# DLRM tower on one core: in the last round one more feature by comparing and multiplying, and half of layer 2 moved behind the last products

## What is computed

```python
e = jnp.stack([tbl_0[ids[:, 0]], ..., tbl_25[ids[:, 25]]], axis=1)        # 2048 x 26 x 128
combined = jnp.concatenate([dense[:, None, :], e], axis=1)                # 27 vectors of a sample
inter = jnp.einsum('bnd,bmd->bnm', combined, combined)[:, TRIU_I, TRIU_J] # 351 products
h = jnp.concatenate([dense, inter, dense], axis=1)
h = jnp.maximum(h @ W_top1 + b_top1, 0.0)                                 # 512 wide
h = jnp.maximum(h @ W_top2 + b_top2, 0.0)                                 # 256 wide
y = h @ W_top3                                                            # one number
```

## Time and profile before

| | us |
|---|---|
| median of 3 runs | 474.87 (474.09 to 474.97) |
| the profiled execution | 477.4 |
| its span on the core | 475.4 |
| PE busy | 416.0 (87%) |
| DVE busy | 337.1 (71%) |
| ACT busy | 214.8 (45%) |
| POOL busy | 399.9 (84%) |

### The profile page before, as it was taken

The page is one execution under the profiler, slowest core; times in us unless marked ns, Lnnn a source line. Parts: engine busy times, 40 slices in busy tenths (PEclk is TensorE's granted clock), DMA queues, the critical chain, the costliest instruction groups (busy, mean ns, idle before and its releaser), DMA issues.

```text
span 475.4 us, 11713 instructions
## 1 busy us (share of the span) xinstructions
PE 416.0 (87%) x4210; PEld 391.8 (82%) x4210; DVE 337.1 (71%) x777; ACT 214.8 (45%) x719; POOL 399.9 (84%) x553
## 2 busy tenths in 40 slices
PE   0546786989999998999999989999699969989898
PEld 0436785989998998989898989999598969879786
DVE  3649878798698858786878769886588846844360
ACT  1044265454555344545544554555245453525352
POOL 7999999899899898998998989989989899899500
PEclk9978898889999999999999999999899998989999
DMA  7984413622221321323133313132132313121100
GB/s 174 219 206 128 114 43 79 160 65 71 72 78 42 79 80 46 78 72 85 41 79 76 80 42 83 48 84 65 40 84 73 79 45 79 44 74 41 29 2 0
DMA packets 19682, 36.58 MB, mean 77 GB/s; under 512 B 7823, under 2 KB 10391, under 8 KB 19630
## 3 DMA queue, kind: packets, MB, share of 16 engines
q0 software_dynamic: 8704, 17.84, 16.7%
q1 hardware_dynamic: 10926, 18.04, 13.3%
HBM read 35.85 MB, written 0.01 MB: 75 GB/s over the span
## 4 chain that ended last, share of the span: by engine, by line
POOL 61%; issue 25%; PE 8%; DMA 1%; POOLq 1%; DVE 1%; ACT 1%; DVEq 0%; ACTq 0%
POOL rows L408 34%; POOL y_wide L397 27%; PE dots_ps L467 2%; PE mlp_ps L506 2%; DMA rows<-in_tbl,idx_sb 1%; DVE inter L866 1%; POOLq L396 1%; PE late_ps L570 1%; PE mlp_ps L515 1%; PE turn_ps L548 1%; PE mlp_ps L557 1%; PE dots_ps L548 1%; ACT inter L690 1%; DMA idx_sb<-in_ids 0%; PE turn_ps L443 0%
## 5 line engine op out<-in xcount | busy, mean ns | idle before, releaser
L408 POOL DMA_INDIRECT rows<-in_tbl,idx_sb x272 | 265.9, 977 | 45.6 <-POOL y_wide L397 43.8
L818 DVE TENSOR_TENSOR onehot<-ids_sb,late_ps 125x1024 fp32r<-125x1024 int32 (+2 forms) x154 | 167.2, 1141 | 10.5 <-DMA ids_sb<-in_ids_by_round 6.5
L866 DVE COPY_PREDICATED inter<-mask,dots_ps 27x48 f32<-27x48 int32 x496 | 103.0, 208 | 79.1 <-ACT inter L690 62.6
L690 ACT COPY inter<-dots_ps 27x64 f32<-27x64 f32 x496 | 99.0, 200 | 92.4 <-PE dots_ps L467 58.7
L397 POOL MEMSET y_wide<- 64x448 f32 x272 | 133.9, 492 | 0.2
L467 PE MATMUL dots_ps<-vecs 128*64 128x54 f32 x1984 | 118.0, 225 | 1.9 <-issue 1.0
L467 PEld LDWEIGHTS dots_ps<-vecs 128*64 128x64 f32 x1984 | 114.0, 140 | 6.5 <-issue 3.4
L483 PE MATMUL turn_ps<-onehot,t_hi 125*128 125x256 f32 x378 | 100.5, 302 | 11.4 <-DVE vecs L646 11.4
L483 PE MATMUL turn_ps<-onehot,t_lo 125*128 125x256 f32 x378 | 96.0, 291 | 0.0
L483 PEld LDWEIGHTS turn_ps<-onehot,t_hi 125*128 125x128 f32 x378 | 75.2, 199 | 15.8 <-issue 10.0
L483 PE MATMUL late_ps<-onehot,t_hi 125*128 125x256 f32 x214 | 60.1, 314 | 22.1 <-DVE t_lo L831 17.2
(11 more groups left out here) (84 smaller groups left out, 364.2 us busy)
## 6 DMA issues: line engine op xcount, KB each, us to landing
ids_sb<-in_ids_by_round SPq DMA_DIRECT2D x25, 375.0 KB
...
```

The lines of the kernel that those rows point to most:

```text
L408: nc.gpsimd.indirect_dma_start(out=rows[v % 2][:, s, :], out_offset=None, in_=tables[f - 1][:, :], in_offset=bass.IndirectOffsetOnAxis(ap= ...
L690: nc.scalar.copy(inter_of(u, q, g, 0, count[g]), products_of(q, g * JG, count[g], place)).then_inc(inter_by_act, 1)
L818: dve.tensor_tensor(part_buffer(k, h)[0:KP, 0:n], home.rearrange("p (o r) -> p o r", o=1).to_broadcast([KP, n, R]), row_of[KT[k]][0:KP, a: ...
L866: dve.copy_predicated(inter_of(u, q, g, a, n), mask[g * 32:g * 32 + N, a:a + n].rearrange("p (j s) -> p j s", s=1).to_broadcast([N, n, QS] ...
```

## The change

One more feature, 25 (table of 1250 rows, 10 blocks), is fetched by comparing and multiplying, for tiles 14 and 15 alone. Its table is loaded in `step((3, 0), ...)` into `t_added`, which lies over the first 10 blocks of `t_lo`, as soon as PE has used the features of the first two tables for the last time; ACT makes `t_hi` of it and DVE `t_lo`. POOL issues no gather of feature 25 for these two tiles (16 in place of 17 each), and group 4 there has one feature. DVE compares for it (`compare_added`, four parts, 10 blocks) in place of the unused `compare(3, 0, 9)` (8 blocks); PE fetches it (`fetch_added`, 20 matmuls) behind the transposes of tile 14; ACT copies it (`copy_added`). SP loads the table (640 KB) and one line of row numbers (128 KB) in place of the last two loads of 375 KB.

At the end, part 1 of layer 2 moves from between groups 3 and 4 of tile 15 to the place of the 14 fillers; 26 of the 32 fillers go; layer 3 of the earlier round moves behind part 0 of the last layer 1, with its ReLU and `keep_y` moved along and its input in a buffer of its own. SP's program and POOL's last pass are written out.

```diff
+        with nc.sbuf_tensor("t_added", [P, LONG * D], F32) as t_added:
+            pass
         t_lo = sb("t_lo", [P, T0[X], D], F32R)
...
-        end_h2_sb = rows[0][:, 0:M2 * R // D, :].rearrange("p s d -> p (s d)").rearrange("p (m r) -> p m r", r=R)
+        first_h2_sb, end_h2_sb = [rows[0][:, a:a + M2 * R // D, :].rearrange("p s d -> p (s d)").rearrange("p (m r) -> p m r", r=R)
+                                  for a in (M2 * R // D, 0)]
...
-        turns += [("rows", 2 * ROUNDS - 2, k) for k in range(NG)] + [("rows", 2 * ROUNDS - 1, k) for k in range(NG)]
+        turns += [("rows", 2 * ROUNDS - 2, k) for k in range(NG)] + [("item", ROUNDS - 1, X)] + [("rows", 2 * ROUNDS - 1, k) for k in range(NG)]
...
+        def gathered_of(tile, k):
+            return [s for s in groups[k] if tile not in LAST_TILES or ORDER[s] != ADDED]
...
+            def load_added(i):
+                sp.wait_ge(onehot_used, halves_made(i, 0, 2))
+                src = tables[ADDED - 1].rearrange("(p t) d -> p (t d)", t=LONG)
+                for a, b in ((0, 112), (112, KP)):
+                    sp.dma_start(t_added[a:b], src[a:b]).then_inc(added_in, 16)
+            def load_ids_added(i):
+                sp.wait_ge(compared, halves_made(i, 0) + H0[2 * NB])
+                sp.dma_start(ids_sb[ids_place(1, 0)][0:KP, 0, :], ids_added[:, :].to_broadcast([KP, R])).then_inc(ids_added_in, 16)
...
+                last = now == (PASSES - 1, 0)
                 load_ids(i, r, 2)
                 refill(i, r * 2)
-                load_ids(i, r, 3)
+                if last:
+                    load_added(i)
+                    load_ids_added(i)
+                else:
+                    load_ids(i, r, 3)
                 if not prev:
                     load_last_w1()
                 refill(i, r * 2 + 1)
                 if not prev:
                     load_w2()
-                load_ids(i, r, 4)
+                if not last:
+                    load_ids(i, r, 4)
                 if prev:
...
-            passes(sp, step, last_step)
+            written_out(step, last_step)
             for r in range(2):
                 sp.wait_ge(out_written[r], 16 + 16 * PASSES)
-            for n in range(LOADS - 1):
-                sp.wait_ge(ids_in[ids_place(1, n * NB)], ids_count(PASSES - 1, 1, n * NB))
...
-                        if ORDER[s]:
+                        if ORDER[s] and not (static(i) and s not in gathered_of(i * 4 + v, k)):
...
-            with pool.Fori(0, PASSES - 1) as i:
+            with pool.Fori(0, PASSES - 2) as i:
                 for v in range(4):
                     gather_tile(i + 1, v)
+            for v in range(4):
+                gather_tile(PASSES - 1, v)
...
+            def fetch_added(i):
+                before = halves_made(i, 1)
+                turn = turn_of["item", ROUNDS - 1, X]
+                bank = turn_ps[turn % 3][:, 0:R]
+                pe.wait_ge(lo_made, split_count(N_PIECES))
+                for h, (a, n) in enumerate(ADDED_PARTS):
+                    pe.wait_ge(compared, before + h + 1)
+                    if h == 0:
+                        pe.wait_ge(*taken(turn - 3))
+                    for t in range(a, a + n):
+                        for part in (t_hi, t_lo):
+                            last = pe.matmul(bank, part[0:KP, t, :], onehot[(before + h) % RING][0:KP, t - a, :],
+                                             start=(t == 0 and part is t_hi),
+                                             stop=(t == LONG - 1 and part is t_lo))
                     last.then_inc(onehot_used, 1)
...
-                stay_busy(mlp_ps[1], 14)
+                layer2(i, 0, 1)
                 for m in range(M1):
+                    if m == 1:
+                        layer3(i, 0, first_h2_sb)
                     for at in range(3 * JG):
                         if at < 2 * JG:
...
                 transpose_rows(i, 2, range(NG))
+                fetch_added(i)
                 layer1(i, 0, 0)
                 dots(i, 2, 0)
                 layer1(i, 0, 1, 2)
@@ -628,20 +679,18 @@
                 transpose_rows(i, 3, (2,))
                 layer2(i, 0, 0)
-                stay_busy(row_ps, 32)
+                stay_busy(row_ps, 6)
                 transpose_rows(i, 3, (3,))
-                layer2(i, 0, 1)
                 stay_busy(row_ps, 4)
                 transpose_rows(i, 3, (4,))
                 dots(i, 3, 0)
                 dots(i, 3, 1, last_dots_ps)
-                layer3(i, 0)
                 end_of_layers(i)
...
+            def copy_added(i):
+                act.wait_ge(onehot_used, halves_made(i, 1) + len(ADDED_PARTS))
+                nc.scalar.copy(vecs[1][:, :, :, NR - 1],
+                               bank_of("item", ROUNDS - 1, X)[:, 0:R].rearrange("p (t b) -> p t b", t=2)).then_inc(fetched, 1)
...
                     split(DENSE_W)
+                if now == (PASSES - 1, 0):
+                    split(N_PIECES)
                 split_input(i, v)
...
                 take_vectors(i, 2, 0, 2, 4)
+                copy_added(i)
                 rectify1(i, 0, 0)
...
                 take_vectors(i, 3, 3)
-                rectify2(i, 0, 0, 1)
                 take_products(i, 3, 0)
                 take_products(i, 3, 1, last_dots_ps)
                 split_input(i, 3, False)
+                rectify2(i, 0, 0, 1, h2_sb=first_h2_sb)
...
+            def compare_added(i):
+                before = halves_made(i, 1)
+                dve.wait_ge(ids_added_in, 16)
+                for h, (a, n) in enumerate(ADDED_PARTS):
+                    dve.wait_ge(onehot_used, before + h - RING + 1)
+                    dve.tensor_tensor(
+                        onehot[(before + h) % RING][0:KP, 0:n],
+                        ids_sb[ids_place(1, 0)][0:KP, 0:1, :].to_broadcast([KP, n, R]),
+                        row_of[LONG][0:KP, a:a + n].rearrange("p (t o) -> p t o", o=1).to_broadcast([KP, n, R]),
                         ALU.is_equal).then_inc(compared, 1)
...
                 take_vectors(i, v + 1, 2)
                 split_input(i, v)
+                if now == (PASSES - 1, 0):
+                    split(N_PIECES)
                 take_vectors(i, v + 1, 4)
...
-                compare(i, r, 9)
+                if now == (PASSES - 1, 0):
+                    compare_added(i)
+                else:
+                    compare(i, r, 9)
...
                 merge_products(i, 3, 1, last_dots_ps)
+                split_input(i, 3, False)
                 keep_y(i, 0)
-                split_input(i, 3, False)
                 keep_y(i, 1, end_ps[0])
```

53 lines of the change are left out of this document (32 added, 21 removed).

## The result

| | before | changed | ratio, 95% interval |
|---|---|---|---|
| median of 20 runs each | 474.80 us | 473.00 us | 0.9971 (0.9959 to 0.9984) |
| the profiled execution | 477.4 | 472.5 | |
| its span | 475.4 | 470.8 | |

The kernel is faster, by 0.3%: 1.4 us by the ratio, 1.8 by the medians. The forecast was 4.0. The changed kernel ran twice more in the experiments, on two chips, at ratios of 0.9958 and 0.9957, so its gain is put at 1.4 to 2.0 us (the three intervals together allow 0.8 to 3.2). Against that stand the two profiled executions, whose spans differ by 4.6 us. Both numbers are true, and what lies between them is the lesson of this case.

A forecast was written before the change was run, and what follows sets the result against it. PE's own queue, fillers included, was taken to set when tile 15's products start, with PE the bound after ACT's split. 4.97 us gained less 1.0 lost gave 4.0 us off 474.87: 470.9 us, range 469.3 to 473.2.

The forecast's parts named there:

- Term 1: Tile 14: the gather wait becomes a 1.1 us wait for DVE's copy, clock stays up; gain 0.2 us.
- Term 2: Tile 15: fewer fillers and moved layer 2 start products at 445.9, last two gathers landing in time; 4.97 us gained in all.
- rival 5: More gain: PE's 1.57 us wait at 442.06 for ACT's ReLU may go; 469.4 us, chance 0.06.
- Term 3: After tile 15's products: 11.03 us to ACT's split stay, moved layer 2 is free, uncovered layer 3 loses 1.0 us.
- Covered work: Splitting the new table, ACT 1.30 and DVE 1.48 us, hides while both wait for PE; written-out POOL pass costs zero.
- rival 3: Cover of the table splits fails in `step((3, 0), ...)`: 2.8 us on PE's path; 473.7 us, chance 0.07.
- Rival 1: Gathers bound tile 15: its last gather takes 5.06 us, products start at 447.25; 472.2 us, chance 0.11.
- Rival 2: Clock falls after a new wait, at tile 14 or before the last layer 1: 1.65 us; 472.5 us, chance 0.12.

The follow-up runs named there:

- e1: The kernel before, profiled again with no edit: ratio 0.9989, profiled span 471.4 us.
- e4: The kernel before without its last 375 KB load of row numbers, SP's program written out: ratio 0.9992.
- e5: The kernel before with only POOL's last pass written out: ratio 1.0004.
- e3: The kernel before with the new end alone, all 17 features still gathered: ratio 1.0051.
- e9: The changed kernel again, unedited, on a third chip: ratio 0.9958 to the kernel before, mean span 471.77 us.
- e13: The changed kernel again, unedited, later on the second chip: ratio 0.9957 to the kernel before, mean span 472.55 us.
- e2: The changed kernel with the old end, so the added feature alone: ratio 1.0005 to the kernel before.
- e15: The changed kernel with layer 3 put back under cover, beside the last layer-1 matmuls, second run: ratio 0.9906 to the kernel before.
- e12: The changed kernel with layer 3 covered and 14 fillers in place of 6 ahead of group 3 of tile 15: ratio 0.9929 to the kernel before.
- e7: The changed kernel with part 1 of layer 2, its ReLUs and layer 3 moved ahead, under cover: ratio 0.9941 to the kernel before.
- e16: The changed kernel with layer 3 covered and no fillers ahead of groups 3 and 4 of tile 15: ratio 0.9935 to the kernel before.

## Why the prediction was wrong, step by step

**What failed is the reading of what sets the start of tile 15's products, and with it the last line of the sum.** The prediction said: "So tile 15 does not wait for gathers: PE's own queue, fillers included, sets when its products start". In the other three profiled executions of a kernel with 17 gathers and the old end, PE's work ahead of the last gather can give only what lies between the two arrivals, and that is next to nothing: the gather sets the start, or comes together with PE. The sum ended: "The profiled execution of before was 2.5 us over the median, so the median should be 474.87 - 4.0." The excess had been seen and was taken as an offset that both kernels share. It was instead the very time that the change takes out: in that execution PE was late against its last gather by 5.83 - 3.71 = 2.1 us, and the 26 fillers and the half of layer 2 lay on the path. (Of the six traces with 17 gathers it alone has the clock at 0.50 behind the wait at tile 14, and it alone has PE's wait of 1.57 us for ACT's ReLU; the others have 0.22 us at most.) In e1 and e4 PE waits for the last gather, 0.56 and 0.34 us, and in e5 the two come together. The ratios say the same of many executions: e3 takes the fillers and the half of layer 2 out alone, and gains nothing. Had the sum been made against the median, it would have had to say: the products start about 3.7 us behind the last gather, before and after. Then what the change gives there is the time of POOL's missing gathers. From e1 to the changed kernel that was 443.18 - 441.78 = 1.4 us; from the mean g of the six executions with 17 gathers (444.62) to the mean of the three changed executions (441.59) it is 3.0, and to the mean of all twelve with 16 gathers (442.26) it is 2.4. Less 0.92 for the tail and what PE-bound executions like e9 and e13 lose (1.0 and 2.6 us by their d - g), this leaves between 0.5 and 2 us, where 1.4 to 2.0 was measured. How often PE is late cannot be told from one profile for each kernel, so the split is an estimate.

**A cost that the sum did not have.** Two gathers fewer, at 1.60 us each, should move the last one by 3.2 us. From the first gather of the last pass to the last one it is 107.9 us on the mean of six executions with 17 gathers and 105.5 on the mean of twelve with 16: 2.4. The 0.8 us between are longer issues, mostly the one beside DVE's split of the added table. "Splitting the new table costs ACT 1.30 and DVE 1.48 us, in a place where both wait for PE" was priced on PE's path alone; on POOL's path, which sets the start of the products in most profiled executions, it was put at nothing.

**The landing.** The gather's landing was estimated well: "2 to 2.6 us after issue"; 443.18 to 445.89 in e1 is 2.7, 441.78 to 444.50 after is 2.7. It was the start of PE that was untypical.

**Term 1** (0.2 us, tile 14). Right in kind: the wait moved from DMA to the copy of DVE (the row names issue; e9 and e13 name DVE's copy, 0.68 and 1.90 us), the clock stayed at 1.00, compares took 3.02 us as forecast. The wait was 0.69 in place of 1.1 us, and group 2 of tile 15 was transposed at 439.00, 0.9 us earlier than before (439.88), where 0.2 was forecast. In the other five executions with 17 gathers, though, the clock did not fall at tile 14 either.

**Term 2** (4.97 with term 1). Against the profile shown it came true: 450.90 to 445.34 is 5.56 us. The 0.6 more is a balance: 0.7 from tile 14 and 1.4 from the wait of 1.57 us, now 0.22, less some 1.5, nearly all of it what the gathers held up. The shorter wait was rival 5, and it is no effect of the change: before has it at 0.22 too (e1), and the changed kernel at 1.38 and 1.48 in e9 and e13. So that the total came near the forecast here is luck. "Both fit, with 1.1 us to spare" failed: PE waited 0.42 and 0.55 us. It came to group 4 at 443.95, 1.05 us earlier than forecast, and the last gather, issued at 441.78 in place of 441.34, was usable at 444.50 in place of 443.9.

**Term 3** (1.0 us lost). Right. The tail went from 22.52 to 23.44, 0.92. From the products to ACT's split it was 10.83 us where 11.03 were forecast, and PE waited 1.04 for it, forecast 1.3. These 0.20 us go with the gather left out, since e2 has them with the old end; the new end by itself costs 1.12 to 1.14. That this is layer 3 is shown by e15 and e12, which take 1.13 us back.

**Covered work.** The splits of the new table stayed hidden from PE: no wait for ACT or DVE behind them in the first profile (rival 3 falls). From POOL they were not hidden (above). Writing POOL's pass out showed no cost (e5). The 640 KB at 375.31 led to no PE wait at group 2 of tile 13. The Trainium skill (DMA: Bandwidth & Descriptors, "Issuing engines are not separate DMA queues") says that DMAs of all engines run on the same 16 DMA engines and interleave. e4 agrees: without the load of 375 KB the last gather of tile 14 no longer holds PE up.

**The rivals.** Rival 1 (gathers bound tile 15) holds in most profiled executions, but by another mechanism than written: the landing is 2.7 us and not 5.06, and it is PE that is earlier. Rival 2 (the clock falls behind a new wait) did not come in the changed kernel's profile at 421 us. It came in e7, e16 and e3 at tile 15, for 1.3 to 2.7 us. Whether it makes the four of 20 executions of the changed kernel with spans of 472.8 to 474.3 us stays open; e13, with PE late from 392 us on, is a second candidate.

**Still open**: whether moving the split of the added table would free POOL; when exactly the clock falls; why PE waits 1.1 to 1.7 us for ACT's ReLU ahead of layer 2 in some executions and not in others; and why e15 is 2.4 us below e13 by their means where the tail explains 1.13.

**A better version.** The changed kernel with layer 3 covered (e7, e15) is ahead of both, at 0.9941 and 0.9906, and e12 at 0.9929 with more fillers. The fillers seem to matter less than the place of layer 3.
